# The second expert layer finishes its rows and scatters them into a buffer of its own, whose token rows are copied to the output at the end

## The reference

```python
    def _L1_ffn_ref(h, gate_w, gate_b, w1, b1, w2, b2):
        ...
        logits = x @ gate_w + gate_b
        probs = jax.nn.softmax(logits, axis=-1)
        idx = jnp.argmax(probs, axis=-1)
        prb = jnp.take_along_axis(probs, idx[:, None], axis=1)[:, 0]
        ...
        kept = pos < C
        ...
        hmid = jax.nn.relu(jnp.einsum('ecd,edf->ecf', buf, w1) + b1[:, None, :])
        ybuf = jnp.einsum('ecf,efd->ecd', hmid, w2) + b2[:, None, :]
        ...
        y_tok = ybuf[idx, pos_g] * (prb * kept)[:, None]
        ...
        y = jnp.nan_to_num(y, nan=0.0, posinf=10000.0, neginf=-10000.0)
    ...
    x = x + _L1_ffn_ref(_layernorm(x, axis=-1)[None], ...)[0]
```

## Time and profile before

| what | us |
|---|---|
| median of 3 runs (5372.53 to 5374.61) | 5372.98 |
| span of the profiled execution | 5371.9 |
| end of the graph part, start of the last layer | 4676 |
| `route` of the last layer starts | 4752 |
| `experts` of the last layer starts | 4798 |
| `combine` starts | 5284 |

### The profile page before, as it was taken

How to read it: one execution, slowest core, us unless ns; L and a number is a source line. 1 busy time by engine, 2 the same in 40 slices (tenths; PEclk the granted TensorE clock), 3 DMA queues, 4 the chain that set the end, 5 groups by cost and what they waited for, 6 DMA issues and landing times. The chain is left out here.

```text
span 5371.9 us, 86748 instructions
## 1 busy us (share of the span) xinstructions
PE 4172.9 (78%) x27330; PEld 3017.8 (56%) x27331; DVE 3413.4 (64%) x7289; ACT 1663.0 (31%) x2903; POOL 2167.4 (40%) x2194
## 2 busy tenths in 40 slices
PE   3477777777777777746999945999999999769992
PEld 2355555555555555534888833666656666458872
DVE  6466666666666666687555577888888888640115
ACT  1233333333333333321222264333333333121121
POOL 1477777777777777700666600000000000202220
PEclk9678777777777887756999966999999999759996
DMA  4766666666666666651566543444444444323333
GB/s 122 189 168 170 167 165 170 170 162 170 170 165 167 170 169 163 158 207 68 193 200 199 183 139 84 81 85 89 81 81 88 87 81 85 88 86 121 100 118 103
DMA packets 946866, 733.83 MB, mean 137 GB/s; under 512 B 703102, under 2 KB 832054, under 8 KB 944599
## 3 DMA queue, kind: packets, MB, share of 16 engines
q1 hardware_dynamic: 835851, 433.62, 31.3%
q0 software_dynamic: 104144, 289.95, 20.0%
q10 hardware_dynamic: 6652, 7.32, 0.4%
HBM read 483.39 MB, written 92.34 MB: 107 GB/s over the span
## 5 line engine op out<-in xcount | busy, mean ns | idle before, releaser
L1288 POOL DMA_INDIRECT gat_rows<-h_rows,gat_sources x1664 | 1577.0, 948 | 509.2 <-issue 485.5
L1526 PE MATMUL gat_sum_ps<-gat_rows,gat_onehot 128*128 128x265 f32 x3328 | 1167.6, 510 | 3.2 <-DVE gat_rows L1418 2.4
L1526 PEld LDWEIGHTS gat_sum_ps<-gat_rows,gat_onehot 128*128 128x128 f32 x3328 | 792.9, 250 | 190.4 <-issue 5.7
L2055 ACT CAST gnn_z<-build_ps 128x392 bf16<-128x392 f32 x992 | 473.4, 486 | 847.7 <-PE build_ps L2070 842.3
L1997 DVE TENSOR_TENSOR onehot_low<-dense_codes,dense_iota_bf 128x2048 bf16<-128x2048 bf16 x496 | 604.0, 1218 | 2.6 <-PE build_ps L2070 2.6
L2080 PE MATMUL back_ps<-zb_pieces,gnn_z 128*128 128x384 bf16 x3038 | 567.1, 327 | 0.0
L2102 PE MATMUL front_ps<-x_res_wide,front_rows 128*128 128x448 bf16 x2604 | 562.5, 353 | 0.0
L1976 POOL DMA_INDIRECT front_rows<-zf_piece_rows,vrow_nodes x62 | 64.8, 1046 | 1231.2 <-PE front_ps L2102 1221.0
L1418 DVE TENSOR_TENSOR gat_rows<-gat_rows,gat_numerators_ps 128x1024 f32<-128x1024 f32 x416 | 502.0, 1207 | 0.0
L2471 PE MATMUL moe_hidden_ps<-moe_rows_T,moe_w 128*128 128x256 f32 (+1 forms) x1408 | 459.9, 483 | 2.7 <-DVE moe_rows_T L2512 0.8
L2070 PEld LDWEIGHTS build_ps<-onehot_high,onehot_low 128*128 128x128 bf16 x7936 | 339.4, 98 | 204.6 <-issue 38.5
(11 more groups left out here) (366 smaller groups left out, 5160.4 us busy)
## 6 DMA issues: line engine op xcount, KB each, us to landing
moe_w<-in_L_ffn_W SPq DMA_DIRECT2D x112, 512.0 KB
gat_targets<-gat_step_targets SPq DMA_DIRECT2D x104, 512.0 KB
moe_w<-in_L_ffn_w SPq DMA_DIRECT2D x32, 1024.0 KB
gat_rows<-h_rows,gat_sources POOLq DMA_INDIRECT x1664
moe_rows_out<-moe_slot_zeros SPq DMA_DIRECT2D x36, 512.0 KB
gat_flags<-gat_tile_flags SPq DMA_DIRECT2D x104, 128.0 KB
normal_rows<-moe_xn_all SPq DMA_DIRECT2D x14, 896.0 KB
mid_taken<-moe_rows_out SPq DMA_DIRECT2D x14, 896.0 KB, 7.3
```

The source lines that it names most:

```text
L1288: pool.indirect_dma_start(out=g[:, b, t, :], out_offset=None, in_=T.h[:, :], in_offset=bass.IndirectOffsetOnAxis(ap=idx[:, b, t:t + 1], ax ...
L1526: last = pe.matmul(po[:, s % BANKS, 0:W], o[:, b, s * SUB + t, :], g[:, b, s * SUB + t, :], start=t == 0, stop=t == SUB - 1)
L2055: nc.scalar.copy(AT[:, k % 2, :, CHUNK * c:CHUNK * (c + 1)], pb[:, c % 2, 0:CHUNK * NT].rearrange("p (u h) -> p h u", u=CHUNK)).then_inc(a ...
```

## The change

The last layer's `combine` goes, and its work moves into the expert block, now a function of its own, `experts_to_output`.

- `project_nodes` of the last layer stores the normal rows into the left half of a new DRAM buffer of 2 KB rows (`T.both`), and after the seven transfers the residual x into the right half (one transfer of 6.4 MB, 1 KB runs), and waits for it.
- SP then stores the token weights to a DRAM column (6272 single values), and x itself to the token rows of `T.out` (6.3 MB and a tail of 106 rows), once the rows of the first two groups have been gathered. Weights are loaded once per expert, eight times in place of sixteen.
- POOL gathers rows of 2 KB (normal and residual side by side, three buffers deep), and for each group also the four columns of token weights.
- Behind the second bias, ACT scales the rows, DVE does the five guard operations and adds the residual row, tile by tile (64 tiles of slots). POOL scatters each tile as it is finished.
- At the end SP waits for all scatters and copies the first 6250 rows of `T.out` to the output, DRAM to DRAM, in two transfers.
- The loop over the groups is written out. The first layer no longer writes zeros for the last one's rows (6.4 MB less of 19.3 MB).

The core of the diff (PE's products and ACT's relu are as before, apart from the names of the semaphores that they wait for):

```diff
...
+    rw = k.sem(f"{tag}_residual_rows_stored") if x_rows is not None else None
...
                     sp.dma_start(xn_rows.rearrange("(i p) d -> p i d", p=P)[:, at, :], xn_all[:, at, :]).then_inc(xs, 16)
+                if x_rows is not None:
+                    sp.dma_start(x_rows.rearrange("(i p) d -> p i d", p=P), x_res[:, :, :]).then_inc(rw, 16)
+                    sp.wait_ge(rw, 16)
                 sp.wait_ge(xs, 16 * (S.NT // GROUP))
...
+def experts_to_output(k, S, C, T, tag, tok, groups, F, func, weight, x_res, out, src_of, dst_of, w1, b1, w2, b2):
...
+    PER = groups // S.NX2
+    DEEP = 3
...
+        xr = k.sb(ctx, f"{tag}_rows", [P, DEEP, Q, 2, D])
+        gw = k.sb(ctx, f"{tag}_slot_weight", [P, 2, Q])
...
+        @block.sync
+        def _(sp):
+            def load(e):
+                b = e % 2
+                if e >= 2:
+                    sp.wait_ge(yc, (e - 1) * PER * Q)
+                sp.dma_start(w1s[:, b, :, :], w1[e, :, :].rearrange("(c p) f -> p c f", p=P)).then_inc(wl[b], 16)
...
+            load(0)
+            sp.dma_start(T.weights.rearrange("(i p) c -> p (i c)", p=P), weight[:, 0, :],
+                         allow_slow_non_contiguous=True).then_inc(sw, 16)
+            for n in range(2):
+                sp.wait_ge(xl[n], 16 * Q)
+            full, tail = rows_of(T.out, S)
+            sp.dma_start(full, x_res[:, 0:NT - 1, :]).then_inc(bw, 16)
+            sp.dma_start(tail, x_res[0:S.TAIL, NT - 1, :]).then_inc(bw, 16)
+            for e in range(1, S.NX2):
+                load(e)
+            sp.wait_ge(bw, 32)
+            for b in range(2):
+                sp.wait_ge(ys[b], 16 * Q * (groups // 2))
+            half = S.N // 2
+            sp.dma_start(out[0:half, :], T.out[0:half, :]).then_inc(st, 16)
+            sp.dma_start(out[half:S.N, :], T.out[half:S.N, :]).then_inc(st, 16)
+            sp.wait_ge(st, 32)
+
+        @block.gpsimd
+        def _(pool):
+            def take(t):
+                if t >= DEEP:
+                    pool.wait_ge(yc, (t - DEEP + 1) * Q)
+                for q in range(Q):
+                    pool.indirect_dma_start(
+                        out=xr[:, t % DEEP, q, :, :].rearrange("p a d -> p (a d)"), out_offset=None, in_=T.both[:, :],
+                        in_offset=bass.IndirectOffsetOnAxis(ap=src_of[:, t * Q + q:t * Q + q + 1], axis=0)).then_inc(xl[t % DEEP], 16)
+
+            def take_weights(t):
+                if t >= 2:
+                    pool.wait_ge(yw, (t - 1) * Q)
+                for q in range(Q):
+                    pool.indirect_dma_start(
+                        out=gw[:, t % 2, q:q + 1], out_offset=None, in_=T.weights[:, :],
+                        in_offset=bass.IndirectOffsetOnAxis(ap=src_of[:, t * Q + q:t * Q + q + 1], axis=0)).then_inc(gl[t % 2], 16)
+
+            def put(t):
+                for q in range(Q):
+                    pool.wait_ge(yc, t * Q + q + 1)
+                    pool.indirect_dma_start(
+                        out=T.out[:, :], out_offset=bass.IndirectOffsetOnAxis(ap=dst_of[:, t * Q + q:t * Q + q + 1], axis=0),
+                        in_=yo[:, t % 2, q, :], in_offset=None).then_inc(ys[t % 2], 16)
+
+            take(0)
+            take(1)
+            pool.wait_ge(sw, 16)
+            take_weights(0)
+            pool.wait_ge(bw, 32)
+            for t in range(groups):
+                if t + 1 < groups:
+                    take_weights(t + 1)
+                if t + 2 < groups:
+                    take(t + 2)
+                put(t)
...
+            def turn(t):
+                b = t % DEEP
+                pe.wait_ge(xl[b], (t // DEEP + 1) * 16 * Q)
+                if t:
+                    pe.wait_ge(tc, t * 2)
...
+            turn(0)
+            for t in range(groups):
+                hidden(t)
+                if t + 1 < groups:
+                    turn(t + 1)
+                outs(t)
...
+            def weigh(t):
+                act.wait_ge(gl[t % 2], (t // 2 + 1) * 16 * Q)
+                for q in range(Q):
+                    act.wait_ge(yb, t * Q + q + 1)
+                    v = yo[:, t % 2, q, :]
+                    nc.scalar.activation(v, v, ACT.Copy, scale=gw[:, t % 2, q:q + 1]).then_inc(yw, 1)
+
+            for t in range(groups):
+                hidden(t)
+                weigh(t)
...
+            def biased(t, q):
+                e = t // PER
+                if t >= 2 and q == 0:
+                    dve.wait_ge(ys[t % 2], (t // 2) * 16 * Q)
+                dve.wait_ge(yp, t * Q + (q + 1))
+                dve.tensor_tensor(yo[:, t % 2, q, :], py[:, q % 2, 0:D], b2s[:, e % 2, :], ALU.add).then_inc(yb, 1)
+
+            def guarded(t, q):
+                n = t * Q + q
+                v = yo[:, t % 2, q, :]
+                dve.wait_ge(yw, n + 1)
+                dve.tensor_scalar(cl[:, :], v, 1e4, -1e4, ALU.min, ALU.max).then_inc(gc, 1)
+                dve.tensor_tensor(ok[:, 0, :], v, v, ALU.not_equal).then_inc(gc, 1)
+                dve.tensor_scalar(ok[:, 1, :], v, 0.0, 0.0, ALU.mult, ALU.not_equal).then_inc(gc, 1)
+                dve.wait_ge(gc, 5 * n + 3)
+                dve.copy_predicated(v, ok[:, 1, :], cl[:, :]).then_inc(gc, 1)
+                dve.wait_ge(gc, 5 * n + 4)
+                dve.copy_predicated(v, ok[:, 0, :], lim[:, :].to_broadcast([P, D])).then_inc(gc, 1)
+                dve.wait_ge(gc, 5 * n + 5)
+                dve.tensor_tensor(v, v, xr[:, t % DEEP, q, 1, :], ALU.add).then_inc(yc, 1)
+
+            turned(0)
+            for t in range(groups):
+                if t + 1 < groups:
+                    turned(t + 1)
+                for q in range(Q):
+                    biased(t, q)
+                    if q:
+                        guarded(t, q - 1)
+                guarded(t, Q - 1)
...
+        T.both = k.dram("normal_and_residual_rows", [S.ROWS, 2 * D])
+        T.out = k.dram("moe2_rows_out", [S.ROWS + S.G2 * TOK2, D])
+        T.weights = k.dram("token_weights", [S.ROWS, 1])
...
-            [T.y1[0:2 * S.ROWS, :], T.y2[0:S.ROWS, :]])
+            [T.y1[0:2 * S.ROWS, :]])
...
-        combine(k, S, "moe2", 1, weight, T.y2, x_res, True, out)
```

160 lines of the change are left out of this document (92 added, 68 removed).

## The result

The changed kernel takes 5324.29 us (median of 4 runs, 5322.22 to 5325.27). The kernel before took 5372.75 us beside it (4 runs), so the ratio is 0.991, with a 95% interval of 0.9896 to 0.9924. The profiled execution took 5324.48 us, with a span of 5322.3 us, 49.6 less than before.

A forecast was written before the change was run, and what follows sets the result against it. It took DVE to bound `combine` and TensorE the expert block; 5371.9 + 18.5 (residual store) + 5.0 (start) - 52.9 (end) = 5342.5 us, median 5343.6. Range 5324 to 5364, the forecast's own 5334 to 5353.

The forecast's parts named there:

- rival A: Final copy: runs as fast as a one-sided transfer, 15.8 us in place of 31.7, kernel 5328 us; chance 0.13.
- Residual store: End of project_nodes: the new 6.42 MB store is on the path in full, +18.5 us, bounds 15.9 and 25.
- Zero stores: First layer: the zero stores that go leave only idle DMA time, 0 us.
- Start of the expert block: Expert block's start: third group's rows wait behind the stored x and token weights, +5 us, bounds 0 and +20.
- the scaling by count: Token-weight store: time taken as 0.79 of a 26.0 us load of 7936 pairs, landing 20.5 us after issue.
- Rival B: Expert block's start: small stores make base rows late and PE idle before turn(2), +20 us, kernel 5359; chance 0.10.
- no engine waits for the token weights: Expert block's start: token weights are gathered by 4829, before their first use at 4833.5, so no wait.
- Steady groups: Expert block's loop: DVE's added 2.33 us a tile is hidden under PE's 28.7 us a group, 0 us.
- The end before the copy: After the last outs: last scatter issued 0.9 us later, copy starts at 5284.45, saved meeting of engines counted as nothing.
- The copy: Kernel's end: 6.40 MB DRAM to DRAM at half of 405 GB/s, 31.7 us plus fixed parts of 2.6 and 0.3.
- wrong if the copy is under 20 us: Final copy: the prediction's own sign that it is wrong, a copy under 20 us or over 45.
- the wrong choice between the two ends: Final copy: bounds 15.8 us if reading and writing overlap, 34.2 if they follow each other; took 31.7, nearer the upper.

The follow-up runs named there:

- e2: The changed kernel with the residual-row store issued at the head of SP's stream in project_nodes, not behind the seven normal-row stores: 5314.85 us, ratio 0.9885.
- E10: The changed kernel with the five guard instructions done twice on every tile: 5349.02 us, ratio 0.9948.
- E1: The changed kernel with its two final copies done once more behind a wait for the first pair: 5353.74 us, ratio 0.9958.
- e6: The changed kernel with its final copy cut into two transfers of 128 x 24 rows of 1 KB and a 106-row tail: 5327.99 us, ratio 0.9921.
- e7: The changed kernel with each half of the final copy issued as 5 x 625 rows of 1 KB: 5361.63 us, ratio 0.998.
- e8: The changed kernel with the token weights stored as 128 runs of 49 values instead of 6272 single values: 5323.07 us, ratio 0.9909.
- e11: Kernel without final copy (both stores heading project_nodes, scatters into the output), with POOL drains behind groups 0, 2, 6 and 14: 5279.23 us, ratio 0.9832.
- e9: Kernel without final copy (both stores heading project_nodes, scatters into the output), with one POOL drain behind the last group but one: 5289.47 us, ratio 0.9836.

## Why the prediction came out as it did

The forecast of 5343.6 us had the right sign and the right places, but was 19.3 us too high. The measured 5324.29 lies 0.3 us inside the range of 5324 to 5364, which had been stretched to take in rival A, and outside the forecast's own 5334 to 5353. The four runs go from 5322.22 to 5325.27, so that it lies inside is luck. What bounds each stage was read rightly; the rate of the copy was not, and the smaller errors had the same sign. Rival A (5328) came nearest, in part by chance: its copy of 18.7 us from issue to the end was 3.6 too short, and the drift and the two ends of the block made up for it.

- **Residual store, +18.5: right.** +18.6 measured, and e2 shows that it is this store alone: moved, 18.5 us return. The bound by 1 KB runs (349 GB/s) was the right row for rows at a pitch of 2 KB.
- **Zero stores, 0: right.** The stretch of the first layer that they shared did not shorten: POOL's wait there is 170.09 us, before 170.02, and the block takes 92.3 us from drain to drain in both.
- **Start of the expert block, +5: right in place and kind, 1.1 too much.** +3.9 measured: outs(0) starts 1.1 later after B, where the forecast had it even (0.4 of it turn(0), 0.7 hidden(0), which runs longer at a granted clock of 0.50), and 2.8 in front of turn(2). The latter was 0.8 to 2.8 in other runs of the same block, so this trace shows a high one. The middle of the sum was nearly right for another reason: the base rows were issued 22.3 us after B, forecast 21.4, but because SP waited 19.9 us for the gathers of two groups, not because an issue was held. The store of the token weights landed after 32.2 us, not 20.5, so the scaling by count fell short by a third, and the base rows beside it landed 50.1 us after B, not 44. The rows of the third group then landed 4.5 us after their last issue in place of 5.5. Rival B's mechanism was at work, at about a seventh of its price. That no engine waits for the token weights was wrong: ACT waited 10.2 us for them, once, which PE did not feel.
- **Steady groups, 0: right.** 2.33 us a tile were forecast for the guard with the add, 2.37 measured. The period is 28.61 us in place of 28.67, so writing out the loop gave the 0.8 us over the block that the prediction had named as the most it could. E10 shows the limit: the cover is nine tenths, since another 7.8 us a group cost 0.7.
- **The end before the copy: 2.7 us off.** From the end of the last outs to the copy's issue it took 7.6 us; before, it was 9.4 us to the first load, and I had forecast 0.9 more. I had counted the saved meeting of engines as nothing. Before, SP's first load of `combine` had to wait until POOL's drain was over (it took 2.0 us there, from 5281.3 on); now SP starts the copy in the same block.
- **The copy, 34.6 us from issue to the end: the step that failed.** Measured 22.3, so 12.3 of the 20.2 us by which the forecast for the span was too high. The step was "in every row one side of the transfer is on chip; here each byte crosses HBM's side twice, and I take half of 405". It does not halve: with 2.6 and 0.3 us of fixed parts as forecast, 19.4 us are left for 6.4 MB, 330 GB/s, and the trace has all bytes within 19 us, at 337. By its own sign ("wrong if the copy is under 20 us") the prediction is wrong here, as the 31.7 us of this term became 19.4. E1 repeats the price (22.1), e6 shows that it is the rate of 1 KB runs as well. Rival A had the mechanism, and its 405 GB/s was too fast by a fifth. The Trainium skill (DMA: Bandwidth & Descriptors, Latency and other measured facts) has 207 and 214 GB/s per direction for copies of 128 x 16 KiB tiles at two row pitches, and less at others. By the prediction's estimate this would have made 30 us. The copies here, contiguous or of 1 KB rows, ran at about 330 GB/s, and for them the measurement decides; leaning on the page would have strengthened the wrong choice between the two ends.
- **Drift, -3.5.** The time up to A moved by more than that from run to run, and 3.4 of it arose before the only place there that the change touches.

By terms: -12.3 (copy), -3.5 (drift), -2.7 (end), -1.1 (start), -0.8 (steady groups), +0.1 (store) make -20.3, against 5322.3 - 5342.5 = -20.2.

## What to carry to other kernels

A stage that only finishes and stores rows was cheap to fold into a stage whose bound is another engine; what decided here is where the extra transfers start: a store of data that was ready cost 18.5 us behind the last store of the stage before, and nothing at its head. Ask next whether the buffer is needed at all: scattering into the output, with the base rows stored there early, saved 14.8 us, and a drain placed in POOL's idle time another 6.7. The kernel with all of it takes 5289.47 us, ratio 0.9836 (0.9822, 0.9849), against 0.991 for the change alone.

## What the runs showed of the hardware

- A copy from DRAM to DRAM ran at about 330 GB/s, each byte counted once, in runs of 50 KB (337 over 19 us) as in runs of 1 KB (e6); cut so that the slowest dimension was 5, it ran at 121 GB/s with a DMA share of 0.34 (e7).
- 6272 single values stored to DRAM took 32.2 us to land in the changed kernel and 9.9 us as 128 runs of 196 bytes (e8). The gathers beside the single values landed 7 us later, and the base rows issued while they were still landing took 4.7 us longer.
- POOL's drain took 2.7 us behind 4 indirect transfers, 3.3 to 3.7 behind 24, 5.2 behind 48, 8.8 behind 92 (e11) and 9.1 behind 188 (e9) since the last drain, but 2.0 behind 128 in the kernel before. So the number alone does not give the time.
